# Splitting B into bf16 parts: the two subtractions go from VectorE to TensorE, and the last copy to ScalarE

## What is computed

```python
x = x + dilate3x3(_gn(x))        # group norm, maximum over 3x3
x = x + mamba(_gn(x))            # tokens: 64 x 64 patches of 4 x 4 x 8 = 128 numbers
x = x + conv3x3(_gn(x), L2) ; x = x + conv3x3(_gn(x), L3)
```

```python
dt, Bc, Cc = split(xc @ x_proj_w.T)          # 8, 32 and 32 rows
dt = softplus(dt @ dt_proj_w.T + dt_proj_b)
h = h * exp(dt * A) + (dt * xc) * Bc         # for every d, s: one step per token
y = sum over s of h * Cc
```

## Time and profile before

| | |
|---|---|
| median of three runs | 14411.47 us (14407.96 to 14422.27) |
| span of the profiled execution, first to last instruction | 14402.8 us |
| busy: DVE, POOL, PE, ACT | 95%, 92%, 87%, 67% of the span |
| mean granted TensorE clock | 0.966 |
| one chunk on average | 110.0 us (14082 us from the first scan to the end of the last, over 128) |

### The profile page before, as it was taken

One profiled execution on the slowest core, in us unless ns is written; L12 is line 12 of the kernel. 1 busy time (PEld: TensorE's weight loads), 2 busy tenths in 40 slices (PEclk: granted clock), 3 DMA queues, 4 the chain that ended last, 5 costly groups with the idle time before them and its releaser, 6 DMA issues.

```text
span 14402.8 us, 165917 instructions
## 1 busy us (share of the span) xinstructions
PE 12558.9 (87%) x28138; PEld 4979.6 (35%) x28138; DVE 13637.5 (95%) x11708; ACT 9660.7 (67%) x18491; POOL 13305.8 (92%) x6039
## 2 busy tenths in 40 slices
PE   5988989888898998989889898898989889899897
PEld 2333333333333333333333333333333333333332
DVE  6999999999999999999999999999999999999995
ACT  5666766666666666666666666676666666666665
POOL 5999999999999999999999999999999999999995
PEclk9999999999999999999999999999999999999999
DMA  3344443434444344443444434444343444434443
GB/s 106 110 124 119 118 124 112 133 109 116 127 114 128 112 117 125 116 127 111 121 122 116 125 110 126 119 118 124 112 132 109 117 126 114 128 112 118 125 116 88
DMA packets 1268462, 1701.57 MB, mean 118 GB/s; under 512 B 403660, under 2 KB 552596, under 8 KB 1267156
## 3 DMA queue, kind: packets, MB, share of 16 engines
q1 hardware_dynamic: 1261572, 1686.16, 40.7%
q10 hardware_dynamic: 5680, 3.15, 0.1%
HBM read 1525.28 MB, written 124.13 MB: 115 GB/s over the span
## 4 chain that ended last, share of the span: by engine, by line
DVE 27%; PE 26%; issue 23%; POOL 12%; DMA 4%; ACT 4%; DVEq 1%; SPq 1%; POOLq 1%; ACTq 0%
DVE h L1368 15%; PE y_ps L1208 15%; POOL hc L709 9%; DVE u_in L1352 8%; PE proj_ps L1149 3%; POOL u_in L683 2%; DMA c_sb<-bc_dram 2%; PE side_ps L1220 2%; DMA raw<-x 2%; PE b_ps L1265 2%; DVE vmax L1331 1%; PE y_ps L1205 1%; ACT a_ps L899 1%; PE side_ps L1194 1%; PE side_ps L1224 1%
## 5 line engine op out<-in xcount | busy, mean ns | idle before, releaser
L709 POOL TENSOR_TENSOR hc<-h,c_sb 128x1024 f32<-128x1024 f32 x4096 | 9607.9, 2367 | 815.5 <-DVE h L1368 703.9
L1368 DVE TENSOR_TENSOR_SCAN h<-a_ps,carry,u_in 128x512 f32<-128x512 f32 x7168 | 8757.6, 1263 | 193.4 <-POOL hc L709 114.3
L1208 PE MATMUL y_ps<-hc,ident 128*128 128x512 f32 x16400 | 8070.1, 617 | 427.4 <-POOL hc L709 420.6
L899 ACT ACTIVATE a_ps<-dt,a_neg 128x512 f32<-128x512 f32 x8192 | 5567.5, 687 | 4121.8 <-DVE h L1368 4069.2
L1208 PEld LDWEIGHTS y_ps<-hc,ident 128*128 128x128 f32 x16400 | 3119.1, 196 | 4031.1 <-issue 2975.8
L1352 DVE TENSOR_TENSOR u_in<-dtx,b_ps 128x1024 f32<-128x1024 f32 x2816 | 3362.9, 1194 | 76.5 <-PE b_ps L1265 44.5
L683 POOL TENSOR_TENSOR u_in<-dtx,b_sb 128x1024 f32<-128x1024 f32 x1280 | 3029.4, 2367 | 0.0
L1265 PE MATMUL b_ps<-b_parts,select 96*128 96x512 bf16 x2816 | 1115.8, 396 | 1039.6 <-DVE u_in L1352 1037.0
L1368 DVE TENSOR_TENSOR_SCAN h<-a_ps,u_in 128x512 f32<-128x512 f32 x1024 | 1200.6, 1208 | 238.8 <-ACT a_ps L899 194.5
L1265 PEld LDWEIGHTS b_ps<-b_parts,select 96*128 96x128 bf16 x2816 | 282.1, 100 | 2540.2 <-DVE u_in L1352 1988.8
L1149 PE MATMUL proj_ps<-u_ln,w_x 128*128 128x512 f32 x2064 | 972.2, 593 | 4.6 <-ACT u_ln L851 3.7
(11 more groups left out here) (129 smaller groups left out, 7438.9 us busy)
## 6 DMA issues: line engine op xcount, KB each, us to landing
c_sb<-bc_dram SPq DMA_DIRECT2D x4100, 256.0 KB, 3.2
b_sb<-bc_dram SPq DMA_DIRECT2D x1282, 256.0 KB, 3.2
z<-x_dram SPq DMA_DIRECT2D x68, 512.0 KB, 8.5
x_dram<-vmax SPq DMA_DIRECT2D x66, 512.0 KB, 4.6
raw<-x SPq DMA_DIRECT2D x129, 256.0 KB
x_dram<-x SPq DMA_DIRECT2D x129, 256.0 KB, 3.8
out<-raw SPq DMA_DIRECT2D x256, 128.0 KB
x<-x_dram SPq DMA_DIRECT2D x128, 224.0 KB, 7.4
```

Of the source, the lines that this page charges most:

```text
L709: pool.tensor_tensor(hc[:, ring_at(c * S + s, HC_RING)], h[:, ring_at(c * S + s, H_RING)], c_sb[:, s // C_GROUP % C_RING, s % C_GROUP:s % ...
L899: act.activation(a_ps[:, a_slot(c * S + s, half)], dt[:, c % 2, half], ACT.Exp, scale=a_neg[:, at:at + 1]).then_inc(a_made, 1)
L1208: mm = pe.matmul(y_ps[:, half], ident[:, :], hc[:, ring_at((c * S + s) % (NC * S), HC_RING), half], start=False, stop=(s == S - 1), skip_g ...
L1368: dve.tensor_tensor_scan(h[:, r, half], a_ps[:, a_slot(c * S + s, half)], u_in[:, s % U_RING, half], start, ALU.mult, ALU.add).then_inc(h_ ...
```

## The change

The two subtractions leave DVE. PE adds `-parts[k]` onto `proj_ps` with a bf16 matmul whose stationary operand is a 32 by 64 matrix, minus the identity in its first 32 columns and zero in the rest; the second time after `split_mid`. ACT copies the last rest into `parts[2]` and raises `proj_emptied`. `rest_done` now counts two per chunk. In PE's program the first subtraction stands in state 18, behind `sum_states` of state 14 and ahead of that state's convolution passes; the second stands in state 20, behind `sum_states` of state 16. In ACT's program the last copy stands in state 19.

```diff
-SPLIT_HI, SPLIT_REST, SPLIT_MID, SPLIT_LO, STORE_C, MOVE_PARTS = 16, 17, 18, 19, 18, 20
+SPLIT_HI, SPLIT_MID, SPLIT_LO, STORE_C, MOVE_PARTS = 16, 18, 19, 18, 20
+LESS_HI, LESS_MID = 18, 20
...
+            act.activation(minus_one[:, :], ident[0:S, 0:2 * S], ACT.Copy, scale=-1.0)
...
             def split_mid(b, c):
-                act.wait_ge(rest_done, chunk(b, c + 1))
+                act.wait_ge(rest_done, chunk(b, c + 1, 2) - 1)
                 act.activation(parts[:, 1, :], proj_ps[0:S, :], ACT.Copy).then_inc(mid_done, 1)
+
+            def split_lo(b, c):
+                act.wait_ge(rest_done, chunk(b, c + 1, 2))
+                act.activation(parts[:, 2, :], proj_ps[0:S, :], ACT.Copy).then_inc(proj_emptied, 1)
...
                         if s == SPLIT_MID:
                             split_mid(b, c)
+                        if s == SPLIT_LO:
+                            split_lo(b, c)
...
+            def subtract_part(b, c, k):
+
+                pe.wait_ge((hi_done, mid_done)[k], chunk(b, c + 1))
+                pe.matmul(proj_ps[0:2 * S, :], minus_one[:, :], parts[:, k, :], start=False, stop=True,
+                          skip_group_check=True).then_inc(rest_done, 1)
...
                         sum_states(b, *behind(c, s, LAG))
+                        if s == LESS_HI:
+                            subtract_part(b, c, 0)
+                        if s == LESS_MID:
+                            subtract_part(b, c, 1)
                         for part, use in tensor_extras(c, s):
                             extra(b, part, use)
...
-            def split_rest(b, c):
-
-                dve.wait_ge(hi_done, chunk(b, c + 1))
-                dve.tensor_tensor(proj_ps[0:S, :], proj_ps[0:S, :], parts[:, 0, :], ALU.subtract).then_inc(rest_done, 1)
-
-            def split_lo(b, c):
-                dve.wait_ge(mid_done, chunk(b, c + 1))
-                dve.tensor_tensor(parts[:, 2, :], proj_ps[0:S, :], parts[:, 1, :], ALU.subtract).then_inc(proj_emptied, 1)
...
-                        if s == SPLIT_REST:
-                            split_rest(b, c)
-                        if s == SPLIT_LO:
-                            split_lo(b, c)
```

More of the change, by code:

```diff
@@ L174, in build @@
         group_z = sb("group_z", [P, P])
+        minus_one = sb("minus_one", [S, 2 * S], BF16)
         halo_keep = sb("halo_keep", [P, 4])
@@ L1017, in _ @@
             split_mid(0, -1)
+            split_lo(0, -1)
             softplus_in(0, -1, 0)
@@ L1256, in _ @@
                     extra(0, part, use)
+                if use[0] == "xproj":
+                    subtract_part(0, -1, 0)
+                    subtract_part(0, -1, 1)
             start_ahead(pe, b_cast)
@@ L1391, in _ @@
             prepare_weights()
-            split_rest(0, -1)
-            split_lo(0, -1)
             start_ahead(dve, u_made)
```

## The result

The changed kernel takes 14470.88 us (median of four runs, 14464.86 to 14484.95) against 14411.88 us (14407.96 to 14422.27) of the kernel before in the same comparison: 1.0042 times as long, 95% interval 1.0027 to 1.0056. It is slower by 59 us; the forecast was 14351 us, 60 us faster, and the range ended at 14394. Its profiled execution has a span of 14463.0 us, 60 us more than the earlier trace rows.

What follows compares the result with a forecast made beforehand. DVE was taken to bound chunks 1 to 4: 77 us gross gain less 16.5 us of waiting on TensorE leaves 60, so 14411.5 - 60 = 14351 us, chance 0.68. The range was 14328 to 14394 us.

Steps and rivals of the forecast that it cites:

- What is taken away: DVE saves 1.20 us per chunk in chunks 1 to 4, 77 us gross over 64 chunks; nothing in the other 64.
- Edits costed at nothing, and their cover: Second subtraction, ACT's copy, `proj_emptied`, chunk 0's wait and steps ahead of the loop: priced at nothing, hidden by existing waits.
- rival 3: Behind the new wait PE falls to its low clock level, about 4.1 us per hit chunk; slower, chance 0.09.
- DVE bounds chunks 1 to 4, a subtraction costs it 0.60 us: In chunks with dilation DVE is busy 109.8 of 110.1 us; each of two subtractions removed saves 0.60 us.
- POOL can follow: POOL waits 0.57 and 0.58 us for DVE after the two subtractions, so has 1.15 us to give there.
- The matmul costs PE 0.50 us: Each new subtraction matmul takes TensorE 0.50 us, between 0.22 and 1.0, including entering and leaving a matmul with few rows.
- late group: 35 chunks with mean 0.63 us to spare before `u_in` of state 20; DVE waits 0.47 us each, 16.5 us.
- early group: 29 chunks with 1.58 to 1.91 us to spare before `u_in` of state 20; needing 1.38 us, they lose nothing.
- PE's wait for `hi_done`: At the first subtraction in state 18, PE stands 0.28 us on average in 29 chunks until `split_hi` ends.
- ACT's copy fits into its wait: ACT's new 0.57 us copy falls into its 1.49 us wait for DVE ahead of the decay of state 21.
- rival 1: All 128 chunks gain 1.20 us, 154 us in all, giving 14258 us; chance 0.05.
- rival 2: TensorE becomes the bound at about 1.3 us per first subtraction; 17 us gain left, 14394 us; chance 0.18.

Runs made afterwards that it cites:

- e3: The kernel before with 128 unused bytes ahead of `x1` and 128 behind it, so only `x1` changes its remainder by 256: 14506.7 us, ratio 1.0070.
- e2: The kernel before with an unused 128-byte tile where the change allocates `minus_one`, so all tiles behind it shift: 14523.0 us, ratio 1.0078.
- e1: The changed kernel with `minus_one` allocated behind all other tiles, so every other tile lies where it lay before the change: 14358.2 us, ratio 0.9962.
- e4: The changed kernel with 128 more unused bytes behind `minus_one`, so tiles behind it lie 256 bytes further than before the change: 14352.5 us, ratio 0.9961.
- e9: The changed kernel with `minus_one` last and two convolution passes moved earlier, from state 16 to 15 and from 18 to 16: 14339.6 us, ratio 0.9951.
- e10: The changed kernel with `minus_one` allocated last, run once more as the base of a later comparison: 14350.0 us, ratio 0.9959.

## Why the prediction was wrong

**The step that failed** is one sentence under "What is taken away": "and nothing from the other 64". The working behind it asked only whether the other chunks could follow an earlier DVE. It did not ask what else in the diff reaches them. Under "Edits costed at nothing, and their cover" stand the second subtraction, the copy, `proj_emptied`, the steps ahead of the loop; the line `minus_one = sb(...)` does not, and the parts of the diff shown ahead of the prediction leave it out too, though it moves every tile behind it, and its 64 bf16 numbers make 128 bytes. The place where it would land was in the rows: in chunk 5 POOL already waited 2.8 us for C. A chunk that waits for a DMA has no cover for a DMA that gets slower, and the same rows that said "no gain here" said "a loss here is paid in full". Measured, chunk 5 went from 108.5 to 114.6 us, 99 us in all. None of the rivals had it; rival 3 had the sign, with another mechanism that did not come. What the address costs: 96 and 112 us in the kernel before (e3, e2), 113 and 118 in the changed one (after less e1, after less e4). Without it the change gains 52 to 62 us (e1 against before in its two comparisons), where 60 was forecast.

The other steps, against the trace of after:

- **DVE bounds chunks 1 to 4, a subtraction costs it 0.60 us.** Right. The scans of chunk 2 still have 0.3 us of idle time, and the distance from state 17 to state 18 falls from 4.06 to 3.48 us on average, 0.58. With the wait at state 20 gone as well (e9), chunks 1 to 3 are 1.19 us shorter. Chunk 4 is only 0.83 us shorter even then: 0.29 us of new idle time stands on average ahead of a scan of its state 28, for which the profile names no releaser. 64 x 1.20 = 77 was thus about 70.
- **POOL can follow.** Right: its 0.57 us after the first subtraction is gone; after the second 0.19 to 0.45 us is left, which goes with the wait at state 20.
- **The matmul costs PE 0.50 us.** Right. PE after, chunk 2, states 18 to 20:

```profile
4868.13 1.88 PE L1224 MATMUL y_ps<-hc,ident 128*128 128x512 f32 x4
4869.94 0.40 PE L1181 MATMUL proj_ps<-parts,minus_one 32*64 32x512 bf16 x1
4870.27 1.13 PE L1236 MATMUL side_ps<-padded,w_main 128*128 128x512 f32 x2
4871.23 1.88 PE L1224 MATMUL y_ps<-hc,ident 128*128 128x512 f32 x4
4872.95 1.91 PE L1240 MATMUL side_ps<-z,ident 128*128 128x512 f32 x2
4874.68 0.40 PE L1284 MATMUL b_ps<-b_parts,select 96*128 96x512 bf16 x1
```

From the first to the fourth line are 3.10 us; four passes and two without it took 1.72 and 0.86, so 0.52 us are the matmul's, though its record says 0.40. The 0.09 us ahead of it and the 0.10 us by which the two passes behind it are longer answer to the entry and exit read off `dt_proj`.

- **The late group loses 0.47 us in 35 chunks, 16.5 us.** Close: `u_in` of state 20 waits in 42 of the 64 chunks, 13.0 us in all. In chunk 2 of image 5:

```profile
4869.88 4.79 DVE L1391 TENSOR_TENSOR_SCAN h<-a_ps,carry,u_in 128x512 f32<-128x512 f32 x4
4875.11 1.22 DVE L1375 TENSOR_TENSOR u_in<-dtx,b_ps 128x1024 f32<-128x1024 f32 x1 [0.44 <-PE b_ps L1284]
```

This chunk had been in the early group. Which group a chunk falls into is not fixed: it depends on how long PE stays at its lower clock level after the idle time ahead of `b_ps` of 16. In the kernel before, the granted clock is at the lower level for 2.8 to 6.1 us between `b_ps` of 16 and that of 20, and over the 64 chunks the spare time at state 20 falls with it, almost on a straight line, from 1.91 to 0.25 us: the two groups of the prediction follow the clock.

- **PE's wait for `hi_done`, 0.28 us in 29 chunks.** Too large: 8 chunks, 1.5 us in all, since in most chunks PE now comes to the place after `hi_done`, as here, at 4869.94.
- **ACT's copy fits into its wait.** Right: ACT stands for PE ahead of the copy in chunk 2, and the decays behind it are in time, since DVE's scans have no new idle time.

```profile
4877.16 0.59 ACT L884 ACTIVATE parts<-proj_ps 32x512 bf16<-32x512 f32 x1 [1.63 <-PE proj_ps L1181]
```

- **Rivals.** Chunks 6 and 7 kept their length, and chunk 5 with `x1` in place too (108.4 against 108.5 us), so rival 1 falls. PE did not become the bound (rival 2): its wait cost 13 us of the 77. (The price of rival 2 counts the new wait twice in the early group: with 0.60 + 1.3 - 1.67 = 0.23 us there, 26 us would be left, not 17.) The clock in chunk 2 is 0.97 against 0.98, and behind the first subtraction PE ran at its higher level in all 64 chunks (rival 3).

## What to carry to other kernels

A diff that allocates a tile moves all tiles behind it; before pricing its instructions, list the start addresses on both sides, and look above all at tiles that DMAs fill in short packets while the DMA engines are full. A chunk that waits for a transfer gains nothing from a faster engine but pays in full for a slower transfer, so "no gain here" needs a second look at what could cost there. And when a result has the wrong sign, compare the stages first: here the forecast gain was all there, in the chunks where it belonged, and the loss stood elsewhere.

## What the runs showed of the hardware

- Packets of 256 bytes into SBUF, many at a time (chunk 5), took 31 to 33 ns on average where the destination of most of them, `x1`, was a multiple of 256, and 49 ns at 128 past one, 48 at 32 past, 44 at 64 past. Few at a time (chunk 6) they took 18 ns either way. With 2048 bytes per packet, 192 past a multiple against in place made no difference that can be told, 107 against 106 ns.
- Over PE's four passes behind `b_ps` of state 16, after 4.5 us without work, the granted clock was below 1 in all 64 chunks (0.5, the lower of its two levels, throughout in 56; e10); after 3.7 us it was below 1 in 53 and 1 throughout in 11 (e9). From start to start a pass took 0.85 us at 0.5 and 0.43 us at 1.
- A bf16 matmul of 32 rows between fp32 matmuls of 128 rows held PE up for 0.52 us, one of two right beside each other for 0.24 us.
